# Two layers of graph, attention and expert networks on one core: root1 cut into pieces between the last weight combinations, its weights loaded from another queue

## The reference

```python
w = einsum('rb,bio->rio', att, basis)     # 30 bases of 512x512 -> 2 relations
for r in (0, 1):
    msgs[r] = sigmoid(x[col] @ gate_w[r])[:, None] * x[col] @ w[r]
agg = segment_sum(where(edge_type == 0, msgs[0], msgs[1]), row)
out = agg + x @ root + bias
```

## Time and profile before

| | us |
|---|---|
| three runs | 994.57, 994.49, 991.76 |
| median | 994.49 |
| the profiled execution's own time | 994.57 |
| its span in the trace | 992.8 |
| busy: TensorE / its weight loads | 934.3 / 610.9 |
| busy: VectorE / ScalarE / GpSimd | 557.6 / 401.1 / 109.5 |
| mean granted clock of TensorE | 0.984 |

### The profile page before, as it was taken

How to read it: one execution, slowest core, us unless ns; L and a number is a source line. 1 busy time by engine, 2 the same in 40 slices (tenths; PEclk the granted TensorE clock), 3 DMA queues, 4 the chain that set the end, 5 groups by cost and what they waited for, 6 DMA issues and landing times. The chain is left out here.

```text
span 992.8 us, 12505 instructions
## 1 busy us (share of the span) xinstructions
PE 934.3 (94%) x4724; PEld 610.9 (62%) x4724; DVE 557.6 (56%) x1176; ACT 401.1 (40%) x670; POOL 109.5 (11%) x98
## 2 busy tenths in 40 slices
PE   3989889999999999999998999989999899999997
PEld 0445444395454494468765656989997644545885
DVE  4798888823147611441315662697876533658861
ACT  3677777311102210111112333478785543424450
POOL 0000000000020213100002000144340000023300
PEclk9999999999999999989999999999999999999899
DMA  9999989560000101062985203222103100230001
GB/s 299 380 392 358 380 332 366 207 218 0 1 21 1 54 20 67 0 223 95 308 288 188 81 1 97 78 64 66 43 1 120 51 1 3 89 85 0 1 1 52
DMA packets 53086, 124.87 MB, mean 126 GB/s; under 512 B 5455, under 2 KB 19539, under 8 KB 53010
## 3 DMA queue, kind: packets, MB, share of 16 engines
q1 hardware_dynamic: 51890, 122.51, 34.6%
q0 software_dynamic: 1120, 1.29, 0.4%
HBM read 120.40 MB, written 3.38 MB: 125 GB/s over the span
## 5 line engine op out<-in xcount | busy, mean ns | idle before, releaser
L412 PE MATMUL PS<-AR 128*125 128x512 f32 (+9 forms) x1394 | 393.9, 440 | 9.0 <-issue 1.9
L412 PEld LDWEIGHTS PS<-AR 128*128 128x128 f32 (+3 forms) x1394 | 212.5, 194 | 168.9 <-issue 161.9
L1951 ACT ACTIVATE AR<-PS 128x500 f32<-128x500 f32 (+6 forms) x73 | 41.9, 578 | 162.4 <-PE PS L412 81.2
L1954 ACT ACTIVATE AR<-iota,AR 125x625 f16<-125x625 f16 x119 | 86.3, 811 | 27.8 <-PE PS L499 27.7
L446 PE MATMUL PS<-AR 128*32 128x512 f32 x420 | 68.1, 628 | 20.8 <-DMA AR<-in_basis 20.5
L1279 DVE TENSOR_SCALAR AR<-iota,AR 125x625 f16<-125x625 f16 x165 | 60.5, 446 | 13.8 <-PE PS L499 13.8
L497 PE MATMUL PS<-AR 125*125 125x512 f16 (+9 forms) x425 | 59.8, 297 | 4.5 <-issue 3.7
L497 PEld LDWEIGHTS PS<-AR 125*125 125x125 f16 x425 | 45.0, 139 | 22.7 <-issue 13.5
L2447 POOL TENSOR_TENSOR whl<-AR,whh 128x512 fp32r<-128x512 f32 x32 | 47.3, 1499 | 90.3 <-ACT whh L1951 90.3
L1799 DVE TENSOR_TENSOR HMl<-AR,HMh 128x626 fp32r<-128x626 f32 x64 | 50.6, 830 | 4.3 <-ACT HMh L1951 4.3
L446 PEld LDWEIGHTS PS<-AR 128*32 128x32 f32 x420 | 15.3, 112 | 57.3 <-issue 39.7
(11 more groups left out here) (320 smaller groups left out, 1512.1 us busy)
## 6 DMA issues: line engine op xcount, KB each, us to landing
AR<-in_basis SPq DMA_DIRECT2D x58, 768.0 KB, 9.4
AR<-in_L_ffn_W SPq DMA_DIRECT2D x20, 1024.0 KB, 7.8
spare<-in_basis SPq DMA_DIRECT2D x22, 768.0 KB, 9.4
AR<-in_L_gnn_Wh SPq DMA_DIRECT2D x8, 512.0 KB, 4.0
AR<-in_L_gnn_Wh SPq DMA_DIRECT2D x16, 256.0 KB, 4.7
AR<-in_L_mix_W_qkv SPq DMA_DIRECT2D x1, 3072.0 KB, 11.4
AR<-in_L_gnn_root SPq DMA_DIRECT2D x2, 1024.0 KB, 14.7
y_dram<-AR SPq DMA_DIRECT2D x8, 256.0 KB, 8.4
```

What stands on the lines that cost most here:

```text
L412: ins = te.matmul(o, l, r, start=start and i == 0, stop=stop and i == len(pairs) - 1)
L1951: return se.activation(o, i, ACT.Copy, scale=scale)
L1954: return se.activation(o, i, f, bias=bias, scale=scale)
```

## The change

`root1` is no longer one piece: its four chunks stand between parts of combinations 14 and 15, and combination 14 goes first. `R1e` becomes one piece of memory in the region `oZ`, from word 12,792 on, loaded by one DMA that ScalarE issues after the last segment is done, in place of four that SyncE issued behind block 32. VectorE does `combo_in(15)` before all five `gx_low` of relation 1, not behind the third.

```diff
-        R1, R1e = ar(oA, 4, 512), [ar(o, 512) for o in (14720, oRING + 5632, oW2 + 1536, oW2 + 3584)]
+        R1, R1e = ar(oA, 4, 512), ar(oZ + 2552, 4, 512)
@@ root1
-                    te.matmul(o, XT[:, k, cols(c)], R1e[k] if c < 4 else R1[:, k, :], start=k == 0, stop=False)
+                    te.matmul(o, XT[:, k, cols(c)], (R1e if c < 4 else R1)[:, k, :], start=k == 0, stop=False)
@@ TensorE, behind the last segment
-            pe.wait_ge(d_r1e, 64)
+            combos(14, 0, 6)
+            pe.wait_ge(d_r1e, 16)
             for s, v in psum.free[0]:
                 pe.wait_ge(s, v)
-            for c in range(4):
-                root1(c, bank[c])
-            combos(14, 0, 12)
+            root1(0, bank[0])
+            combos(14, 6, 12)
+            root1(1, bank[1])
+            combos(14, 12)
             u = psum.take("many", "dve", slot=2)
             slot(u)
             pe.wait_ge(many_ready, 1)
             te.matmul(sl(u.slot, 0, 10, 1), ones[0:P, 0:1], sm[0:P, 3, 0:2, 0:5], start=True, stop=True).then_inc(u.sem, 1)
-            combos(14, 12)
-            combos(15)
-            psum.at = 2
+            root1(2, bank[2])
+            combos(15, 0, 6)
+            root1(3, bank[3])
+            combos(15, 6)
             psum.held.discard(3)
@@ VectorE
             for c in range(NT):
                 gx_low(0, 0, c, c + 1)
-            for c in range(NT):
-                if c == 3:
-                    combo_in(15)
+            combo_in(15)
+            for c in range(NT):
                 gx_low(0, 1, c, NT + c + 1)
@@ ScalarE, in the loop over segments
                     ac.wait_ge(seg_done, g + 1)
+                    if g == NS - 1:
+                        se.dma_start(R1e, A["L0_gnn_root1"].rearrange("(k p) n -> p k n", p=128)).then_inc(d_r1e, 16)
                     for b in range(NT):
@@ SyncE, in the loop over basis blocks
-                if n == 32:
-                    for k in range(4):
-                        ye.dma_start(R1e[k], A["L0_gnn_root1"][128 * k:128 * k + 128, :]).then_inc(d_r1e, 16)
```

## The result

The changed kernel is slower: 1004.75 us (median of 12 runs, 998.96 to 1007.88) against 996.39 (12 runs, 991.76 to 1000.04). The ratio is 1.009, 95% interval 1.0069 to 1.0111: 6.9 to 11.1 us. The prediction of 997.3 with 993.8 to 1000.5 missed it. Of the 7.4 us between 997.3 and 1004.75, 1.8 are its base: it was put on 994.57, and twelve runs of before have the median 996.39. The rest is the change: +8.4 by the medians, where +2.75 was forecast. The profiled execution took 1003.82, its span is 1002.0, against 994.57 and 992.8.

What follows compares the result with a forecast made beforehand. TensorE, busy 94% of the span, was taken as the bound, the z units' start setting the end. Order +2.7 and R1e's load +0.05 made 2.75 us on 994.57: 997.3 us, range 993.8 to 1000.5.

Steps and rivals of the forecast that it cites:

- What goes: Around combinations 14 and 15, TensorE's waits for ScalarE and the last blocks go: 1.4 + 2.1 = 3.5 us saved.
- 1, a new wait in front: Combination 14, now first, waits for VectorE's `w_ready` 14, so TensorE starts 2.65 us later.
- split rounds: Combinations 14 and 15, cut into parts, take 12 rounds in place of 10: 1.72 us more.
- ends: Five more changes of shape between root1 and combination pieces, 0.13 to 0.16 us each: 0.75 us.
- the run behind "many": Remaining root1 chunks and combination 15's parts run from 187.24 to z units at 200.13, against 197.44: +2.7 us.
- 4, "many" becomes a wait: At the small "many" matmul TensorE stands 0.7 us for VectorE, some 1.0 with the matmul itself.
- The issue on ScalarE: R1e's DMA issue ahead of the flush's copies delays them and what follows by 0.4 us; bounds 0 to 0.74.
- The early megabyte: Near 80 us the stream loses 1 MB: combination 6 gains 0.35 us, combination 7's gain is lost to the flush.
- Does R1e arrive?: At half the bandwidth R1e takes 7.4 us, landing at 173.4, before root1 wants it at 175.7.
- Moved for nothing: `combo_in(15)` ahead of `gx_low` costs nothing: VectorE finishes 5 to 6.5 us into the z units, relation 1 wanted after 11.6.
- The rival on the clock: Half clock after the new gap ahead of combination 14 costs 1.4 to 3.3 us, giving 998.0 to 999.9; chance 0.18.
- The rival on R1e: Blocks already queued go first, R1e lands at 183, 7.3 us late, z near 206.5: 1004 us; chance 0.04.

Runs made afterwards that it cites:

- e1_order: Against the kernel before: new order of TensorE and VectorE, but R1e loaded early by SyncE and the second bias later; ratio 1.0027 (1.0004 to 1.0049).
- e5_order_fill: e1_order with 13 matmuls of zeros between the flush and combination 14; ratio to the kernel before 1.0009 (0.9992 to 1.0026).
- e3_rows8k: The kernel after with R1e read in rows of 8 KB in place of 2 KB; ratio to the kernel before 1.0027 (1.0011 to 1.0044).
- e9_rows1k: The kernel after with R1e in two DMAs of half the columns, rows of 1 KB; ratio to the kernel before 1.0123 (1.0085 to 1.0162).
- e8_gap: e1_order with combo_in(13) one chunk later on VectorE; ratio to the kernel before 1.0064 (1.0038 to 1.0089).
- e6_early: The kernel after with R1e issued behind segment 22, not 24, and eight words further in memory; ratio to the kernel before 1.0028 (1.0001 to 1.0054).

## Why the prediction was wrong

Step by step, in the prediction's own order:

- *What goes.* Right: no wait for ScalarE or for the last blocks remains in the kernel after.
- *1, a new wait in front.* Right in kind and releaser, too short: 3.87 us, where 170.96 to 173.82 and the 0.4 of the issue make 3.3. The missing 0.6 is combination 13: I had taken its end from a run in which it waited for its last block, 5.1 us behind the segment's end (170.96 - 165.81); with its blocks there, it is 4.6 (169.52 - 164.91). That wait was cover, and it was gone. It is scatter at least in part: e1_order had the wait, e5_order_fill did not.
- *2, 3, 5, split rounds, ends, the run behind "many".* Right: from the second part of combination 14 on the pieces cost 1.85, 3.63 and 3.56 in the kernel after, and e1_order and e5_order_fill give the whole at +2.4 for a forecast of +2.7.
- *4, "many" becomes a wait.* Right in kind where nothing else is late, smaller than the 0.7 forecast (0.39 in e1_order, 0.20 in e5_order_fill). In the kernel after it is the other way: VectorE waits 7.34 us for "many".
- *The issue on ScalarE.* Right: 0.42 us, and the copies start 0.70 us behind the segment's last matmul and not 0.23; 0.4 was taken.
- *The early megabyte.* Right: combination 6's 0.35 is gone (4.48 us from 88.78), combination 7 still takes 5.56 (from 97.16), and the flush starts at 100.16 as before.
- *Does R1e arrive?* This step failed. I had 7.4 us; it took 14.6, and root1(0) waited 2.80 us for it. Half the bandwidth was assumed because two queues take turns. e3_rows8k, e9_rows1k and the counts of packets show turns by packet, one row each, so that the share follows the row length, a quarter here; the latency beside a full stream is 2.2 us more. The Trainium skill (DMA: Bandwidth & Descriptors, on arbitration) states the turns "at *packet* granularity", and the equal counts agree; turning that into half the bytes was my error.
- *Moved for nothing.* Right: TensorE is busy for all 86.5 us from 206.5 to 293.
- *The rival on the clock.* It had 0.18 and happened. Priced as 1.4 to 3.3 us less the slack, it cost 1.8 in 14a (3.63 against 1.85) and 3.0 in root1(0) (6.64 against 3.6). Without the second stand, in e3_rows8k, root1(0) lost 0.9 (4.5 against 3.6) behind the same 3.63 in 14a, so 2.1 of the 3.0 go with that stand. The Trainium skill (TensorE: Matmul & The Clock Gate, Part 1) has activity lift the clock; this trace agrees, with 0.50 held over the wait for R1e and 1.00 from 186 on, 6 us of work behind it. In e9_rows1k the clock came back at 177 (1.00 in 177 to 178), at the end of 14a, and fell again in the gap of 9.50.
- *The rival on R1e.* It had 0.04, and its mechanism was wrong: no queueing behind the blocks, a wait of 2.80 us, not 7.3. That its 206.5 and 1004 meet the measured 206.43 and 1003.82 is luck; the clock made up the rest.

The sum of what was mis-sized, in the stage over e1_order: 1.8 + 3.0 + 2.8 = 7.6 us and 0.5 for the later `w_ready` 14, less 0.6 for "many" and the stand there, makes 7.5; measured 41.5 - 34.1 = 7.4. The two rivals were taken as alternatives with a chance each. Here they came together and lengthened each other, for both bear on the stage in which TensorE has nothing else to do; so their chances and prices could not be added as they were. With the clock fallen but R1e early (e8_gap) the stage is 37.3, and with R1e's rows of 8 KB 36.4: 4.2 to 5.1 us of the 41.5, more than half of those 7.4, go with the late R1e.

Open: whether the clock falls here in every execution of the kernel after; each trace shows one. The mean granted clock of its 21 executions on record has the median 0.978 (0.973 to 0.986), and 0.983 in e1_order's ten (0.981 to 0.984), so a fall in most of them is likely and one in all is not shown. Open too is the length of gap that lets the clock fall.

## What to carry to other kernels

Before a block of work is moved out of a place where TensorE would else wait, find what it covered there, and take the other waits of that profile as gone when sizing the gap: a gap of some 4 us cost the clock behind it as well. A transfer on a second queue, beside a saturated stream of 6 KB rows, got a share by its row length; ask for it early, or give it long rows. When two rivals hit the same stage, price them together too. Fill the wait with a piece of the moved work, and cut combinations only where a round ends.

## What the runs showed of the hardware

- Two DMA queues at once, beside a stream of 6 KB rows: both moved the same number of packets (330 and 328 in 6 us of the kernel after), so 1 MB landed in 9.5, 14.6 to 15.4, and 21.1 us with rows of 8, 2 and 1 KB. No packet of the second queue moved in the first 2.9 us behind its issue in the kernel after, and none in the first 1.9 in e6_early.
- The granted clock fell to 0.50 behind every gap of 3.82 us or more in this stretch, and behind neither of 1.51 and 2.72 in one profile each; matmuls of zeros kept it at 1.00.
- A DMA issued by an idle ScalarE took 0.42 us and put that engine's next work back by 0.47. In e6_early the issue (158.60) ran beside an activation, and the next one started at 158.67.
